# Attention projections of a sandwich layer on one core: eight block products and steps of 512 tokens, or seven block products and windows of 1024 tokens

## The reference, cut to what matters

```python
x = x + _layernorm(attn(_layernorm(x)))        # x: 2 batches x 1024 tokens x 512, float32
x = x + _layernorm(ffn(_layernorm(x)))         # SwiGLU over 1792 hidden units, ternary integer weights
# attn: 32 heads of 128, blocks of tokens in order
qkv = silu(hidden @ qkv_w.T)                   # qkv_w: 12288 x 512
scores = einsum('bhnd,bhmd->bhnm', cq, ck) * diag_decay
intra = einsum('bhnm,bhmd->bhnd', scores, cv)
inter = einsum('bhnd,bhde->bhne', cq * q_decay, kv)
kv_next = kv * block_decay + einsum('bhnd,bhne->bhde', ck * k_decay, cv)
xf = attn * rsqrt(mean(attn * attn) + EPS)     # over the 4096 values of a token
out = (sigmoid(hidden @ gate_w.T) * norm_w * xf) @ out_w.T
```

## Time and profile before

| | before |
|---|---|
| profiled execution: its time, its span | 2612.68 us, 2610.9 us |
| PE (TensorE matmul) busy | 2559.8 us, 98% of the span, 14560 matmul records |
| PEld (TensorE weight load) busy | 2219.7 us, 85% |
| DVE (VectorE) busy | 1161.5 us, 44% |
| ACT (ScalarE) busy | 816.5 us, 31% |
| POOL (GpSimd) busy | 849.6 us, 33% |
| DMA | 149.41 MB, mean 57 GB/s |
| granted TensorE clock, mean | 0.996 of full |

### The profile page before, as it was taken

How to read it: one execution, slowest core, us unless ns; L and a number is a source line. 1 busy time by engine, 2 the same in 40 slices (tenths; PEclk the granted TensorE clock), 3 DMA queues, 4 the chain that set the end, 5 groups by cost and what they waited for, 6 DMA issues and landing times.

```text
span 2610.9 us, 39939 instructions
## 1 busy us (share of the span) xinstructions
PE 2559.8 (98%) x14560; PEld 2219.7 (85%) x14560; DVE 1161.5 (44%) x2073; ACT 816.5 (31%) x1251; POOL 849.6 (33%) x585
## 2 busy tenths in 40 slices
PE   7999999999999999999999999999999999999996
PEld 6888888888888888888888888888888888777774
DVE  6334444444334434343334444444344345655558
ACT  5232323222322222222322232223222225643333
POOL 3232333232323223232323332323232233434345
PEclk9999999999999999999999999999999999999998
DMA  4111212121111112121112121211111121101001
GB/s 162 40 62 54 69 49 72 48 72 42 63 48 60 57 49 65 50 72 41 60 52 68 50 73 50 73 45 60 48 61 55 42 71 65 54 25 41 31 25 65
DMA packets 77985, 149.41 MB, mean 57 GB/s; under 512 B 11216, under 2 KB 43984, under 8 KB 77008
## 3 DMA queue, kind: packets, MB, share of 16 engines
q1 hardware_dynamic: 71856, 137.20, 15.5%
q10 hardware_dynamic: 6048, 11.01, 1.4%
HBM read 110.43 MB, written 37.75 MB: 57 GB/s over the span
## 4 chain that ended last, share of the span: by engine, by line
PE 87%; issue 6%; DVE 3%; POOL 3%; ACT 1%; DMA 0%; POOLq 0%; SPq 0%; ACTq 0%; DVEq 0%
PE proj_ps L1218 55%; PE yp L1218 15%; PE sc_st L1259 4%; PE at_ps L1280 4%; PE at_ps L1283 4%; PE sc_st L1269 4%; POOL h_lo L452 2%; PE at_ps L1218 1%; DVE stats L807 1%; POOL d_lo L447 0%; DVE y L1156 0%; PE sc_st L1226 0%; ACT y L528 0%; POOL f_lo L442 0%; ACT L569 0%
## 5 line engine op out<-in xcount | busy, mean ns | idle before, releaser
L1218 PE MATMUL proj_ps<-x_hi,w_hi 128*128 128x512 f32 x1536 | 621.9, 405 | 3.4 <-DVE k L867 2.0
L1218 PE MATMUL proj_ps<-x_hi,w_lo 128*128 128x512 f32 x1536 | 606.3, 395 | 0.0
L1218 PE MATMUL proj_ps<-x_lo,w_hi 128*128 128x512 f32 x1536 | 605.8, 394 | 0.0
L389 POOL TENSOR_TENSOR sumsq<-sumsq,sq 128x512 f32<-128x512 f32 x128 | 164.6, 1286 | 1180.7 <-ACT sq L584 1180.5
L912 DVE TENSOR_TENSOR y<-yp,y 128x512 f32<-128x512 f32 x256 | 177.0, 691 | 475.7 <-PE yp L1218 475.7
L1218 PEld LDWEIGHTS proj_ps<-x_hi,w_lo 128*128 128x128 f32 x1536 | 288.6, 188 | 68.4
L1218 PEld LDWEIGHTS proj_ps<-x_hi,w_hi 128*128 128x128 f32 x1536 | 289.3, 188 | 61.0 <-issue 2.2
L1218 PEld LDWEIGHTS proj_ps<-x_lo,w_hi 128*128 128x128 f32 x1536 | 289.5, 188 | 58.0
L1218 PE MATMUL proj_ps<-w_hi,x_hi 128*128 128x256 f32 x1024 | 294.2, 287 | 2.0 <-DVE q L867 2.0
L1218 PE MATMUL proj_ps<-w_hi,x_lo 128*128 128x256 f32 x1024 | 288.9, 282 | 0.0
L1218 PE MATMUL proj_ps<-w_lo,x_hi 128*128 128x256 f32 x1024 | 288.5, 282 | 0.0
(11 more groups left out here) (121 smaller groups left out, 4320.4 us busy)
## 6 DMA issues: line engine op xcount, KB each, us to landing
raw<-w_attn SPq DMA_DIRECT2D x64, 512.0 KB, 3.2
k_blocks<-sq SPq DMA_DIRECT2D x64, 512.0 KB, 2.6
k_tok<-k_blocks SPq DMA_DIRECT2D x256, 128.0 KB, 2.9
check<-w_ints ACTq DMA_DIRECT2D x42, 256.0 KB, 2.6
ow<-w_out SPq DMA_DIRECT2D x16, 512.0 KB, 3.3
fraw<-w_ints SPq DMA_DIRECT2D x7, 1024.0 KB, 4.8
table_stage<-tables SPq DMA_DIRECT2D x16, 258.0 KB, 3.0
x_again<-x SPq DMA_DIRECT2D x4, 1024.0 KB, 5.5
```

The source lines that it names most:

```text
L389: pool.tensor_tensor(sumsq[:, tokens(seg)], sumsq[:, tokens(seg)], sq[:, h], ALU.add).then_inc(ss_done, 1)
L1218: last = pe.matmul(psum, s, m, start=n == 0, stop=n == len(terms) - 1)
```

## The change

Each kind (K, Q, V, gate) of a pair and a batch of 1024 tokens is now one 2 by 2 by 2 block product: rows of blocks are the two heads, columns the two halves of the batch (512 tokens each), and the contraction is split in two. It is formed by seven products in place of eight (Winograd's form): `product` is 6 matmuls of 512 columns, and 28 of them make a window, which takes the place of two steps. There are 32 windows, the 16 pairs on the first batch and then again on the second.

- The second operands of the seven products (`xb`: three blocks of x and four sums, high and low) are made once for each batch, the second batch's during window 0, kept in HBM and loaded in window 15.
- The first operands need sums of weight blocks: POOL's `combine_weights`, four additions of 128 by 256 for each kind and window, then `split_hi_a`/`split_lo_a` (three blocks, 128 by 768) and `split_hi_s`/`split_lo_s` (the four sums, 128 by 1024). Two slots of `raw`, `w_hi` and `w_lo` serve the four kinds in turn, so all weights are loaded and split in each window, twice as often as before.
- The seven products sum up in three banks (chains). ScalarE keeps the first (`keep_s1`), VectorE adds the rest: `keep_s2`, `keep_s3`, `finish_22`, `finish_12`, `finish_21`, five additions for each kind. Only one of the four results is still in PSUM when its sigmoid is taken; for K, Q and V the other three are multiplied in SBUF with the sigmoid in `zz`, both operands in SBUF.
- V is projected feature-major too, written to HBM as blocks, read back into `kv_tok` (which K's blocks and the output weights use as well) and turned by VectorE (`turn_v`).
- The sums of squares, `y` and `table` are held for one batch; `w_out` is loaded and split in each window. The attention's output of the first batch is saved to HBM. The last window's attention and the feed-forward part no longer overlap.

The diff, cut to what the window consists of:

```diff
+B_11, T_2, T_3, B_21, T_1, B_22, T_4 = range(7)
+A_11, A_12, A_22, S_1, S_2, S_3, S_4 = range(7)
+A_21 = 3
+NB = 7
+FACTORS = {1: (A_11, B_11), 2: (A_12, B_21), 3: (S_4, B_22), 4: (A_22, T_4),
+           5: (S_1, T_1), 6: (S_2, T_2), 7: (S_3, T_3)}
+CHAIN = {1: 0, 2: 0, 6: 1, 5: 1, 3: 1, 7: 2, 4: 2}
...
+ORDER = [(KK, 1), (KK, 6), (KK, 7), (KK, 2), (KK, 5), (QQ, 1), (KK, 3), (KK, 4),
+         (QQ, 6), (QQ, 7), (QQ, 2), (QQ, 5), (VV, 1), (QQ, 3), (QQ, 4),
+         (VV, 6), (VV, 7), (VV, 2), (VV, 5), (GG, 1), (VV, 3), (VV, 4),
+         (GG, 6), (GG, 7), (GG, 2), (GG, 5), (GG, 3), (GG, 4)]
...
         @block.sync
...
-            def swap_blocks(n):
-                sp.wait_ge(blocks_done, 2 * n + 2)
-                wait(sp, kd_done, 2 * n)
-                sp.dma_start(k_blocks.rearrange("i t b n -> (i t) (b n)"),
-                             kt.rearrange("p b h c d -> p (b h c d)")).then_inc(kt_out, 16)
-                sp.wait_ge(kt_out, 16 * (n + 1))
-                for b in range(QUADS):
-                    sp.dma_start(k_tok[quad(b)].rearrange("t i h c d -> t i (h c d)"),
-                                 k_blocks[:, :, b].rearrange("i t n -> t i n")).then_inc(kt_in, 16)
+            def weights(w, kind, pair):
+                wait(sp, wlo_a_done, kinds_until(w, kind) - 2)
+                sp.dma_start(raw[:, kind % 2], w_attn[pair, kind]).then_inc(raw_in[kind % 2], 16)
+            def out_weights(a, pair):
+                sp.wait_ge(v_done, 4 * a + 4)
+                sp.dma_start(ow, w_out[pair]).then_inc(ow_in, 16)
...
+            def window(w, pair, next_weights=True, second_batch=False, attn_save=False):
+                a = w - 1
+                weights(w, GG, pair)
...
+                    weights(w + 1, KK, pair + 1 if not isinstance(pair, int) else (pair + 1) % PAIRS)
+                k_write(w, 1)
+                k_read(w, 1)
+                k_write(w, 0)
+                if next_weights:
+                    weights(w + 1, QQ, pair + 1 if not isinstance(pair, int) else (pair + 1) % PAIRS)
+                k_read(w, 0)
+                v_write(w, 1)
+                v_write(w, 0)
+                v_read(w, 0)
+                if next_weights:
+                    weights(w + 1, VV, pair + 1 if not isinstance(pair, int) else (pair + 1) % PAIRS)
+                v_read(w, 1)
+                if next_weights:
+                    pair_table(w + 1, pair + 1 if not isinstance(pair, int) else (pair + 1) % PAIRS)
...
         @block.gpsimd
...
+            def combine_weights(w, kind):
+                done = 4 * kinds_until(w, kind) - 4
+                slot = kind % 2
+                pool.wait_ge(raw_in[slot], 32 * w + 16 * (kind // 2) + 16)
+                wait(pool, wlo_s_done, kinds_until(w, kind) - 1)
+                pool.tensor_tensor(ws[:, 0], raw[:, slot, A_21], raw[:, slot, A_22],
+                                   ALU.add).then_inc(s_step, 1)
+                pool.tensor_tensor(ws[:, 2], raw[:, slot, A_11], raw[:, slot, A_21],
+                                   ALU.subtract).then_inc(s_step, 1)
+                pool.wait_ge(s_step, done + 1)
+                pool.tensor_tensor(ws[:, 1], ws[:, 0], raw[:, slot, A_11],
+                                   ALU.subtract).then_inc(s_step, 1)
+                pool.wait_ge(s_step, done + 3)
+                pool.tensor_tensor(ws[:, 3], raw[:, slot, A_12], ws[:, 1],
+                                   ALU.subtract).then_inc(s_step, 1)
...
+            def window(w, first=False, next_weights=True, rms_of=None):
+                a = w - 1
+                split_out_lo(a)
+                combine_weights(w, VV)
+                split_lo_s(w, VV)
+                split_lo_a(w, VV)
+                gated_lo(a, 0, 0)
+                gated_lo(a, 0, 1)
+                add_squares(a, 0, 0, first)
+                add_squares(a, 0, 1)
+                combine_weights(w, GG)
+                query_decay(w, 0, 0)
+                split_lo_s(w, GG)
+                split_lo_a(w, GG)
+                add_squares(a, 1, 0, first)
+                if next_weights:
+                    combine_weights(w + 1, KK)
+                query_decay(w, 0, 1)
+                add_squares(a, 1, 1)
+                query_decay(w, 1, 0)
+                query_decay(w, 1, 1)
+                gated_lo(a, 1, 0)
+                gated_lo(a, 1, 1)
+                if next_weights:
+                    split_lo_s(w + 1, KK)
+                    split_lo_a(w + 1, KK)
+                    combine_weights(w + 1, QQ)
+                    split_lo_s(w + 1, QQ)
+                    split_lo_a(w + 1, QQ)
...
         @block.scalar
...
+            def window(w, next_weights=True, checks=None):
+                a = w - 1
...
+                keep_s1(w, KK)
+                sigmoid(w, KK, OUT11)
+                keep_s1(w, QQ)
+                split_out_hi(a)
+                split_hi_s(w, VV)
+                sigmoid(w, KK, OUT22)
+                square(a, 0, 0)
+                gated_hi(a, 0, 0)
+                split_hi_a(w, VV)
+                sigmoid(w, KK, OUT12)
+                sigmoid(w, KK, OUT21)
+                square(a, 0, 1)
+                gated_hi(a, 0, 1)
...
+                sigmoid(w, QQ, OUT11)
+                keep_s1(w, VV)
+                sigmoid(w, QQ, OUT22)
+                k_decay(w, 1, 0)
+                k_decay(w, 1, 1)
+                split_hi_s(w, GG)
+                sigmoid(w, QQ, OUT12)
+                split_hi_a(w, GG)
+                sigmoid(w, QQ, OUT21)
+                square(a, 1, 0)
+                k_decay(w, 0, 0)
+                k_decay(w, 0, 1)
+                square(a, 1, 1)
+                sigmoid(w, VV, OUT11)
+                gated_hi(a, 1, 0)
+                gated_hi(a, 1, 1)
...
         @block.vector
...
+            def keep_s2(w, kind):
+                dve.wait_ge(proj_done, products_until(w, kind, 6))
+                dve.wait_ge(s1_done, kinds_until(w, kind))
+                dve.tensor_tensor(projected(kind, OUT21), blocks_view(kind, chain(kind, 1)[:, :]),
+                                  projected(kind, OUT12), ALU.add).then_inc(s2_done, 1)
+            def keep_s3(w, kind):
+                dve.wait_ge(proj_done, products_until(w, kind, 5))
+                dve.tensor_tensor(projected(kind, OUT22), blocks_view(kind, chain(kind, 1)[:, :]),
+                                  projected(kind, OUT12), ALU.add).then_inc(s3_done, 1)
...
+            def silu(w, kind, out_block):
+                dve.wait_ge(sig_done, outs_until(w, kind, out_block))
+                dst = projected(kind, out_block)
+                src = blocks_view(kind, chain(kind, 0)[:, :]) if out_block == OUT11 else dst
+                dve.tensor_tensor(dst, src, blocks_view(kind, zz_slot(kind, out_block)),
+                                  ALU.mult).then_inc(silu_done, 1)
...
+            def window(w, first=False, checks=None, rms_of=None):
+                a = w - 1
...
+                keep_s2(w, KK)
+                update_state(a, 0, 0)
+                silu(w, KK, OUT11)
+                update_state(a, 0, 1)
+                keep_s3(w, KK)
+                scale_out_weights(a)
+                finish_22(w, KK)
+                finish_12(w, KK)
+                gate(a, 0, 0)
+                silu(w, KK, OUT22)
+                finish_21(w, KK)
+                keep_s2(w, QQ)
+                silu(w, KK, OUT12)
+                silu(w, KK, OUT21)
+                gate(a, 0, 1)
+                turn_k(w, 1, 0)
+                turn_k(w, 1, 1)
...
+                silu(w, QQ, OUT11)
+                update_state(a, 1, 0)
+                keep_s3(w, QQ)
+                turn_k(w, 0, 0)
+                finish_22(w, QQ)
...
+                gate(a, 1, 1)
+                silu(w, VV, OUT11)
+                add_out(a, 3, first)
+                keep_s3(w, VV)
+                finish_22(w, VV)
...
         @block.tensor
...
-                kind = (KK, QQ, VV, GG)[u // 2]
-                split_product(proj_ps[h][:, :],
-                              [(w_hi[:, kind, r, h], w_lo[:, kind, r, h]) for r in range(HT)],
-                              [(x_hi[:, r, tokens(seg)], x_lo[:, r, tokens(seg)]) for r in range(HT)],
-                              proj_done)
+            def product(w, kind, i, x_wait=False):
+                n = kinds_until(w, kind)
+                if i == 1:
+                    pe.wait_ge(wlo_a_done, n)
+                    wait(pe, c21_done, n - 2)
+                if i == 6:
+                    pe.wait_ge(wlo_s_done, n)
+                    if kind == KK:
+                        wait(pe, sig_done, outs_until(w - 1, GG, OUT11))
+                    else:
+                        pe.wait_ge(silu_done, silus_until(w, kind - 1, OUT11))
+                if i == 7:
+                    wait(pe, c12_done, n - 1)
+                if i == 2:
+                    pe.wait_ge(s1_done, n)
+                if i == 5:
```

(44 more changed lines are left out.)

1977 lines of the change are left out of this document (1199 added, 778 removed).

## The result

| | us |
|---|---|
| before, median | 2611.53 |
| after, median of 4 (3042.00 to 3052.28) | 3048.31 |
| ratio, 95% interval | 1.1669 (1.1648 to 1.1690) |
| forecast (range) | 2829 (2625 to 2920) |
| profiled execution after, its span | 3052.28, 3050.5 |

The kernel became slower, as forecast, but by 437 us and not by 217, outside the range. First lines of the page, after: busy times, TensorE's granted clock in 40 slices, and two groups of instructions (busy us, mean ns of one, idle time before them and what ended it).

What follows compares the result with a forecast made beforehand. TensorE bounds the kernel before; after, strict-order waits: 72.8 by order + 1.2 locks + 1.6 clock = 75.6 us a window against 69.6. 2610.9 + 31 x (75.6 - 69.6) + 31 = 2828 us of span; forecast 2829, range 2625 to 2920.

Steps and rivals of the forecast that it cites:

- TensorE's work, 64.0 us a window: Sum of TensorE's matmul work in one window if it never waits, 5.6 us below the 69.6 of two steps.
- The two waits in series: TensorE waits ahead of (QQ, 3), starting at 28.4 not 24.8, then (VV, 3), 8.8 us late; the first adds 5.
- Steps 1 to 3: Window start: POOL's combine of V's weights ends at 17.4 us, holding ACT's split and square; first gate at 20.2, not 14.8.
- Step 4: ACT's and DVE's lists after the first gate: turns of K done at 25.2 us, keep_s3 of Q at 28.4.
- the locks: K's silus with two SBUF inputs held up by running POOL operations: 0 to 2.4 us a window, 1.2 taken.
- The clock: Granted clock drops to its lower level after the wait at (VV, 3): 0 to 1.6 us a window, 1.6 taken.
- Step 8: SyncE loads next Q weights after POOL's low parts, then reads K's second half: landed at 48.1 us; up to 1 later.
- step 6: ACT, held in k_decay until K's first half lands, works to 36.6 us; last silu of Q on DVE at 38.0.
- locks, clock and queued reads in full: Rival: all three at full price, windows of 77.8 us, edges at their upper ends, 2930 us; chance 0.12.
- The edges: Outside the repeating windows: window 0 +6, last attention and feed-forward +20, second batch's operands +5, together +31 us.
- The chance of 0.13 for "faster": Chance that the changed kernel beats the kernel before by more than 0.2%, most of it near 2590 us.
- if TensorE never waits, 64.0 and 2468: Rival's extreme case: windows of 64.0 us, kernel 2468 us; within the 0.13 in all for its rival.

Runs made afterwards that it cites:

- Experiment 11: Experiment 10 plus POOL writing the low parts of the gate's weights ahead of the query decay, window 0 included: 2561.1 us, 0.9808 of the kernel before.
- experiment 1: Changed kernel with SyncE reading K's second half ahead of loading the next Q weights: 3006.5 us.
- experiment 5: Changed kernel with POOL combining V's weights ahead of the low parts of the output weights: 2906.1 us.
- experiment 8: Changed kernel with only ACT's second request for a block of integers moved behind K's decays: 3017.6 us.
- Experiment 4: Changed kernel with 20 filler matmuls ahead of (QQ, 3) and 24 ahead of (VV, 3) in each window: 3016.5 us.
- Experiment 10: The four moves together, plus the last attention put ahead of the first batch's norms, residuals and loads: 2598.0 us, 0.9948 of the kernel before.
- four moves together: Changed kernel with V's combine first, K's second half read first, gated low parts early, integers' request behind K's decays: 2603.0 us.
- experiment 2: Changed kernel with ACT's split_hi_s of V moved behind the square and the first gated head's high part: 2978.0 us.
- experiment 12: Changed kernel with three moves in POOL's list alone: V's combine first, G's low parts first, gated low parts early: 2707.5 us, 1.0366 of before.

## Why the prediction was half right

**TensorE's work, 64.0 us a window: right to 1 us.** Experiment 11 has windows of 63.96 in the second batch, with 0.95 of it a wait ahead of (QQ, 3), so the work is 63.0. The 5.6 us of gain per window were real, and order alone hid them.

**The two waits in series: right in place, cause and sequence.** (VV, 3) waited 5.5 us and (QQ, 3) 4.7 in the first batch, each released by the `keep_s3` named. By the moves that the steps imply, experiment 1 took the first away and experiment 5 brought 6.9 us of waits up to (QQ, 3) down to 3.2. Steps 1 to 3 were right to 0.2 us.

**Step 4 failed first**, by 3.6 us. For the locks the prediction took 1.2, the middle of 0 and 2.4, with the argument that POOL is busy 46 of 73 us. It was 2.4, the upper end: in a window that repeats, a meeting is no matter of chance. The rule of the Trainium skill cited there (SBUF — State Buffer, "Who interferes with whom") had pointed to that end. The 2.4 are read from durations in the trace; no run takes the locks away alone. The other 1.2 us are ACT's wait for DVE's look at the integers, which stands in both lists and was not followed; experiment 8 prices it at 2.5 us a window of the first batch.

**The clock was counted once, at (VV, 3), with 1.6 us.** It was 2.4 to 2.5 us, and it came at (QQ, 3) too, where it also held up `split_hi_a` of G. The price was taken from a stretch of matmuls of 256 columns; twelve of 512 columns at 0.427 in place of 0.227 give the right one. Experiment 4 shows that not all of it lies on the path.

**Step 8 took nothing for reads behind a 512 KB load** and named up to 1 us as the bound. They cost 1.3 (5.5 in place of 4.2), and 0.3 more went by ahead of their issue. Beside them the last silu of step 6, 1.1.

Summed: 72.8 by the order alone, 2.4 for the locks, 1.2 for the integers, 1.1 for the last silu, 0.2 for POOL's low parts, 1.6 for step 8 and 2.5 for the clock at (VV, 3) make 81.8. The forecast had 75.6 and its upper bound 78.5. The rival "locks, clock and queued reads in full" had each of these causes, at 77.8, and lacked the second clock drop and the wait for the integers.

**The edges: 96 us in place of 31.** The prediction gave window 0 an end at 90 with +6; the next window began near 125. It had weighed what window 0 lacks and not followed its lists: from K's second product on TensorE waits there in ten places, 0.3 to 6.4 us each, 36 us together. Behind the last score it took 439.8 us in place of 370.1 + 20. Experiment 10 moved the attention ahead of the norms and won 2.7 us there, so that order explains little of the tail; which part of it the chain of engine changes costs stays open. At window 0, too, only the order of G's low parts was tried, for 1.2 us. So of the 65 us that the edges cost beyond the forecast, what the waits are is read from the trace, and no experiment shows what they are worth. The +5 for the change of batch was short as well, 90.2 us where its neighbours take some 80, but that stands in the mean of the windows.

**The chance of 0.13 for "faster"** was given to this kernel, not to its idea. The rival "if TensorE never waits, 64.0 and 2468" has the windows of experiment 11. With that run's edges, 98 us in place of 31, it comes to 2535; experiment 11, with windows of 64.8, 76.2 at the change of batch and 95.5 behind window 0, to 2561.

What the profile after was to show came out: PE at 84%, the two waits with their releasers, POOL ahead of `qd`, ACT ahead of `kd` and of `split_hi_s`, SyncE ahead of its load, silus at 1.5 to 1.6 us, a clock of 0.92. Only the windows, 79 to 82 us, lay above the 73 to 78. That PE's share came out as forecast is luck in part: at the lower clock a matmul counts as busy for longer, so PE is busy 69.5 of the window's 81.8 us for 64 us of work.

## What to carry to other kernels

Where no engine is full and every list is strict, removing one wait gives its length less what the next one takes back (42 us for experiment 1, 445 for four moves together), so follow the lists to the end of the loop before pricing, and move what is waited for (experiment 5, 142 us), not the waiter (experiment 2, 70 us). In a loop that repeats exactly, price a possible collision as always or never, by where the two operations lie.

## What the chip showed that was not expected

- A DVE `tensor_scalar` with one input, from SBUF to SBUF, is held up by a running POOL operation as the two-input product is: 1.33 us on average against 0.43 beside an idle POOL, the pair in the rows 0.28 us behind POOL's end. The two-input product lasts 0.68 or 0.69 beside an idle POOL and 1.3 to 2.5 beside a busy one, in the changed kernel nearly the same at each place of the window every time. With one input in PSUM it lasted 0.68 in 32 of 32 meetings.
- In the stretches behind waits of 4.7 and 5.5 us the granted clock was 0.50 and 0.51; in the one with a wait of 1.5 us it was 1.00. Matmuls that only fill the two long waits kept it at 1.00 in the stretch shown, and more work on TensorE made the kernel 32 us faster (experiment 4).
- Four reads of 128 KB, issued right behind a 512 KB load, took 5.5 us from the first issue to the engine that waits for them, against the 4.2 that the prediction took from the earlier trace rows. From the first issue to the last landing the median over all windows is 5.4 us behind a load (experiment 12 the same) and 4.2 in experiment 1, where the reads go out ahead of it.
